# Layer 3 of the first batch: experts by scattered blocks instead of all experts for all tokens

## The reference

```python
qkv = xn @ w_qkv.T; q, k, v = split(qkv, 3)             # 64 wide, causal
s = softmax(mask(q @ k.T / 8)) @ v @ w_out.T + b_out
logits = xn @ router_w.T
topk_scores, topk_idx = top_k(logits + router_bias, 2)   # 2 of 16 experts
topk_scores = softmax(topk_scores)
hidden = silu(gate_all) * up_all                         # 16 experts, 64 hidden each
out = sum over the two experts of topk_scores * (hidden @ down)
out = out + (silu(xn @ sh_gate.T) * (xn @ sh_up.T)) @ sh_down.T
x = x + s * silu(out)
```

## Time and profile before

| what | us |
|---|---|
| median of three runs | 745.58 |
| span of the profiled execution | 753.9 |
| layer 3 of batch 0 | about 437.9 to 536.3 |
| layer 2 of batch 1 | about 536.3 to 659 |
| layer 3 of batch 1 | about 659 to the end |
| TensorE busy | 668.3 (89%) |
| VectorE busy | 433.6 (58%) |
| ScalarE busy | 365.3 (48%) |
| GpSimd busy | 196.9 (26%) |

### The profile page before, as it was taken

The page is one execution under the profiler, slowest core; times in us unless marked ns, Lnnn a source line. Parts: engine busy times, 40 slices in busy tenths (PEclk is TensorE's granted clock), DMA queues, the critical chain, the costliest instruction groups (busy, mean ns, idle before and its releaser), DMA issues. The chain is left out here.

```text
span 753.9 us, 12248 instructions
## 1 busy us (share of the span) xinstructions
PE 668.3 (89%) x4114; PEld 424.1 (56%) x4114; DVE 433.6 (58%) x940; ACT 365.3 (48%) x845; POOL 196.9 (26%) x194
## 2 busy tenths in 40 slices
PE   6899899994996899898998899899797998799896
PEld 2785434793783766665665654345365665645353
DVE  1826654561341753673575758765685486566654
ACT  4311683531661644356648643345348568453331
POOL 2000074036046100474555700000036334500000
PEclk9956997996998799996999999999999999999999
DMA  8800031252442431010000000000000000000000
GB/s 316 313 1 0 0 98 56 71 173 88 143 138 69 127 95 57 27 28 0 2 22 9 2 0 1 14 1 1 15 1 1 2 1 1 2 1 0 15 1 14
DMA packets 24044, 35.95 MB, mean 48 GB/s; under 512 B 2792, under 2 KB 14800, under 8 KB 23472
## 3 DMA queue, kind: packets, MB, share of 16 engines
q1 hardware_dynamic: 21008, 27.95, 11.2%
q0 software_dynamic: 2976, 7.21, 3.4%
HBM read 25.98 MB, written 9.18 MB: 47 GB/s over the span
## 5 line engine op out<-in xcount | busy, mean ns | idle before, releaser
L1157 ACT ACTIVATE arena<-bank 128x512 f32<-128x512 f32 (+8 forms) x224 | 125.7, 565 | 145.7 <-PE bank L544 63.8
L544 PE MATMUL bank<-arena,w 128*64 128x128 f32 (+2 forms) x528 | 150.1, 431 | 12.5 <-ACT arena L1157 6.6
L1157 ACT ACTIVATE arena<-bank,arena 128x128 f32<-128x128 f32 (+1 forms) x244 | 87.6, 386 | 108.5 <-PE bank L544 56.8
L544 PE MATMUL bank<-arena 64*128 64x256 f32 (+8 forms) x832 | 119.2, 346 | 2.4 <-ACT arena L1157 2.3
L544 PE MATMUL bank<-arena,work 128*128 128x128 f32 x624 | 88.2, 289 | 13.6 <-ACT arena L1157 4.7
L544 PEld LDWEIGHTS bank<-arena 64*128 64x128 f32 (+4 forms) x832 | 79.8, 181 | 31.8 <-issue 14.5
L544 PE MATMUL bank<-xn_b,w 128*128 128x512 f32 (+1 forms) x192 | 93.0, 608 | 4.8 <-DVE arena L2358 3.5
L544 PEld LDWEIGHTS bank<-arena,work 128*128 128x128 f32 x624 | 80.1, 200 | 27.5 <-issue 22.5
L544 PEld LDWEIGHTS bank<-arena,w 128*128 128x128 f32 (+1 forms) x528 | 62.4, 165 | 50.7 <-issue 34.8
L2448 POOL DMA_INDIRECT slots_in<-arena x32 | 33.8, 1055 | 99.1 <-ACT arena L1157 89.6
L544 PEld LDWEIGHTS bank<-xn_b,w 128*128 128x128 f32 (+1 forms) x192 | 35.0, 192 | 42.9 <-issue 29.5
(11 more groups left out here) (223 smaller groups left out, 912.8 us busy)
## 6 DMA issues: line engine op xcount, KB each, us to landing
work<-in_ew SPq DMA_DIRECT2D x46, 256.0 KB
slots_in<-work SPq DMA_DIRECT2D x2, 1472.0 KB, 17.4
arena<-slots_in SPq DMA_DIRECT2D x10, 256.0 KB, 4.1
slots_out<-arena POOLq DMA_DIRECT2D x10, 256.0 KB, 2.8
w_ew<-in_ew SPq DMA_DIRECT2D x1, 2048.0 KB, 11.7
w<-in_p SPq DMA_DIRECT2D x1, 1840.5 KB, 9.8
w<-in_p SPq DMA_DIRECT2D x1, 1297.0 KB, 10.5
w<-in_p SPq DMA_DIRECT2D x1, 1092.0 KB
```

The costliest lines, as they stand in the source:

```text
L544: return nc.tensor.matmul(o, lhsT, rhs, start=start, stop=stop, skip_group_check=True)
L1157: return nc.scalar.activation(o, i, f, bias=bias, scale=scale, **kw)
```

## The change

Layer 3 of batch 1 stays as it was. Layer 3 of batch 0 becomes `layer3_first`, and its experts leave it:

- `layer3_first` has 13 slots (`SLOTS3`). They hold the eight attention tiles, the shared expert of both groups, routing of both groups, `T1` and `N1` (table `SIDE3`), the transposes of the normalised tokens into rows (`rows_of`), a counting of tokens by expert (`counted`, nine matmuls) and, on VectorE, `dispatch3`: the place of each token's two rows in 31 blocks of 128, and a table of each block's expert (`table3`). The 16 routed experts are not computed there.
- GpSimd scatters 16 times 128 rows into `slots3_in` (DRAM) ahead of its layer-2 work of batch 1. SyncE blanks `slots3_in` at the start of the kernel.
- The 31 blocks are computed in eight groups of up to four (`experts3`, stream `X0`), ten advances, from within `layer2_att` of batch 1: after steps m = 2, 3, 4, 5, 6, 8 of g = 0 and m = 2, 4, 6, 8 of g = 1 (`X_AT`).
- Weights of each block come from DRAM, with register values read from `table3`.
- GpSimd gathers the results by token after its layer-2 work of batch 1, and a last stream `Y0` (`tail3`) forms batch 0's output inside `layer3(1)` of batch 1.

```diff
+X_AT = ((2, 3, 4, 5, 6, 8), (2, 4, 6, 8))
+Y_AT = (1, 2, 3, 4, 5)
...
+                def load_weights3(q):
...
+                    if q >= 2:
+                        sp.wait_ge(*at_of(0, "eo3", q - 2))
+                    for k in blocks3(q):
+                        e = nc.values_load(table3[0:1, 0, k:k + 1], engines=[mybir.EngineType.SP], min_val=0,
+                                           max_val=(E3 - 1) * H3)
+                        if q % 2:
+                            for a in range(2):
+                                sp.dma_start(ring3[1][:, k % SB3, (1 - a) * H3:(2 - a) * H3],
+                                             gate_up[:, a, bass.ds(e, H3)]).then_inc(ring3_in[1], 16)
+                        else:
+                            sp.dma_start(ring3[0][:, k % SB3].rearrange("p (a c) -> p a c", a=2),
+                                         gate_up[:, :, bass.ds(e, H3)]).then_inc(ring3_in[0], 16)
+                        half = nc.values_load(table3[0:1, 1, k:k + 1], engines=[mybir.EngineType.SP], min_val=0, max_val=1)
+                        pair = nc.values_load(table3[0:1, 2, k:k + 1], engines=[mybir.EngineType.SP], min_val=0,
+                                              max_val=(EP3 - 1) * D)
+                        sp.dma_start(dring3[sides3(q)[1], k % SB3],
+                                     downs[bass.ds(half, 1), :, bass.ds(pair, D)].rearrange("a h c -> (a h) c")).then_inc(
+                                         ring3_in[q % 2], 16)
...
+                for q in range(2):
+                    load_weights3(q)
+                sp.wait_ge(scattered3, 16 * 4 * C)
+                for q in range(2):
+                    load_slots3(q)
+                for q in range(NSB3 + 1):
+                    if q + 2 < NSB3:
+                        load_slots3(q + 2)
+                    if 1 <= q and q + 1 < NSB3:
+                        load_weights3(q + 1)
+                    if q:
+                        store_rows3(q - 1)
...
+                    def inward(q):
+                        o = fresh("quick", "gu3", q)
+                        pe.wait_ge(*at("cols3", q))
+                        pe.wait_ge(ring3_in[q % 2], (48 if q % 2 else 32) * sum(len(blocks3(j)) for j in range(q % 2, q + 1, 2)))
+                        for j, k in enumerate(blocks3(q)):
+                            i = mm(o[:, cs(j)], ring3[q % 2][:, k % SB3], cols3[:, q % 2, cs(j)])
+                        i.then_inc(*step("gu3", q))
+
+                    def outward(q):
+                        o = fresh("quick", "eo3", q)
+                        pe.wait_ge(*at("hx3", q))
+                        for j, k in enumerate(blocks3(q)):
+                            i = mm(o[:, cs(j)], hx3[sides3(q)[1], cs(j)], dring3[sides3(q)[1], k % SB3])
+                        i.then_inc(*step("eo3", q))
+                    for s in range(NSB3 + 2):
+                        if s < NSB3:
+                            turned(s)
+                        if 1 <= s <= NSB3:
+                            inward(s - 1)
+                        if s >= 2:
+                            outward(s - 2)
+                        yield
...
@@ layer2_att @@
+                        if now[1] and m in X_AT[g]:
+                            advance("X0")
```

More of the change, by code:

```diff
@@ L993, in entry3, with score3 @@
                     i.then_inc(*step("v3", g))
+                sums_at = {}
+                def score3(n):
+                    g = n // C
+                    halves = (n + 4) // 4
+                    pe.wait_ge(*at("k3", g))
+                    for k in range(halves):
+                        keys = min(GT, (n + 1) * CT - k * GT)
+                        o = fresh("quick", "s3", n, k)
+                        last = k == halves - 1
+                        half = slice(k * DK, (k + 1) * DK)
+                        i = mm(o[:, 0:keys], q3[half, n * CT:(n + 1) * CT], k3[half, k * GT:k * GT + keys],
+                               stop=not last)
+                        if last:
+                            i = mm(o[:, keys - CT:keys], identb[:], above[:], start=False)
+                        i.then_inc(*step("s3", n, k))
@@ new lines, in values3 @@
+                def values3(n):
+                    g, c = n // C, n % C
+                    if c == 0 and now[1] == 0:
+                        sums_at[g] = fresh("slow", "o3", g)
+                    for k in range((n + 4) // 4):
+                        pe.wait_ge(*at("pt3_s", n, k))
+                        for j in range(min(4, n + 1 - 4 * k)):
+                            i = mm(sums_at[g][:, c * DK:(c + 1) * DK], pt3[:, k, j], v3[:, 4 * k + j],
+                                   start=k == 0 and j == 0, stop=4 * k + j == n)
+                        i.then_inc(*step("pv3", n, k))
+                    if c == C - 1:
+                        reached[("o3", g)] = reached[("pv3", n, k)]
+                        growing.discard((now[1], "o3", g))
@@ new lines, in probs3 @@
+                def probs3(n):
+                    halves = (n + 4) // 4
+                    needs = [("mx3", n)]
+                    if n >= 2:
+                        needs.append(("pt3", n - 2, (n + 2) // 4 - 1))
+                    after(*needs)
+                    for k in range(halves):
+                        keys = min(GT, (n + 1) * CT - k * GT)
+                        fn(p3b[:, n % 2, k * GT:k * GT + keys], psum("s3", n, k)[:, 0:keys], ACT.Exp,
+                           bias=sm3[:, n, 0:1], accum_out=sm3[:, n, 1 + k:2 + k]).then_inc(
+                            *step("e3", n, k))
+                        reached[("s3", n, k, "read")] = reached[("e3", n, k)]
@@ new lines, in turned3 @@
+                def turned3(n):
+                    halves = (n + 4) // 4
+                    for k in range(halves):
+                        kc = min(4, n + 1 - 4 * k)
+                        after(("pt3", n, k), *([("pv3", n - 1, (n + 3) // 4 - 1)] if n else []))
+                        fn(pt3[:, k, 0:kc], psum("pt3", n, k)[:, 0:kc * CT].rearrange(
+                            "p (a b) -> p a b", b=CT), ACT.Copy).then_inc(*step("pt3_s", n, k))
+                        reached[("pt3", n, k, "read")] = reached[("pt3_s", n, k)]
@@ L2083, in entry2, with experts3, inner, evicted @@
                         pass
[L2085 removed]
+                def experts3():
+                    def inner(q):
+                        n = len(blocks3(q)) * P
+                        low, high = sides3(q)
+                        dve.wait_ge(*at("tg3x", q))
+                        if q == 0:
+                            dve.wait_ge(*at_of(1, "x", 2, 1))
+                        v.scalar_tensor_tensor(t3x[high, 0:n], tg3x[low, 0:n], 1.0, psum("gu3", q)[low, 0:n], ALU.add,
+                                               ALU.mult).then_inc(*step("t3x", q))
+                        after(*([("eo3", q - 2)] if q >= 2 else []))
+                        v.scalar_tensor_tensor(hx3[high, 0:n], t3x[high, 0:n], 0.5, psum("gu3", q)[high, 0:n], ALU.mult,
+                                               ALU.mult).then_inc(*step("hx3", q))
+                        reached[("gu3", q, "read")] = reached[("hx3", q)]
+                    def evicted(q):
+                        n = len(blocks3(q))
+                        dve.wait_ge(*at("eo3", q))
+                        if q >= 2:
+                            dve.wait_ge(rows3_out_sem[q % 2], 16 * (q // 2))
+                        v.tensor_copy(rows3_out[:, q % 2, 0:n], psum("eo3", q)[:, 0:n * P].rearrange(
+                            "p (b d) -> p b d", d=P)).then_inc(*step("rows3_out", q))
+                        reached[("eo3", q, "read")] = reached[("rows3_out", q)]
+                    for s in range(NSB3 + 2):
+                        if 1 <= s <= NSB3:
+                            inner(s - 1)
+                        if s >= 2:
+                            evicted(s - 2)
+                        yield
@@ L2087, in expert_blocks @@
+                advance = streams(dict(F=front, S=shared, C=nothing, M=mamba, T=tail, N=entry2, G=nothing, X=experts3,
+                                       Y=tail3), now)
                 def expert_blocks():
```

609 lines of the change are left out of this document (470 added, 139 removed).

## The result

The changed kernel takes 814.7 us (median of four runs, 808.8 to 823.1) against 745.3 for the kernel before: a ratio of 1.095 (95% interval 1.085 to 1.106). The direction of the forecast was right; its 765 us was 50 short and the range ended at 790. Some executions of most kernels are slower by some per cent at a lower granted clock (one each of e12 and e16 took over 1000 us), so medians here are of all executions and ratios with their intervals of the faster ones alone; for e3, e14 and e18, with two of those each, there is none.

What follows compares the result with a forecast made beforehand. TensorE was taken to bound layer 3 of batch 0, SyncE's weight loads to decide. 753.9 - 44 + 18 - 2 + 39.9 + 5 + 3 = 773.8 us of span, by 0.989: 765 us, range 730 to 790.

Steps and rivals of the forecast that it cites:

- What bounds it, and where the change is decided: TensorE bounds layer 3 of batch 0; SyncE's new weight loads in batch 1's attention decide the change.
- 1, dense experts removed: Layer 3 of batch 0: removing the experts saves 49.3 us of TensorE and 33 us of VectorE work.
- 2, what is left in layer 3 of batch 0: The stage falls from 98.4 to 54 us, -44 (-50 to -36); staying over 70 would show the prediction wrong.
- 3, the blocks: Batch 1's attention: 31 blocks add 18.0 us of TensorE work, of which 2 fall into existing waits.
- 4, the stalls: Batch 1's attention: five waits for SyncE's weight loads cost 39.9 us (30.4 with low prices, 56.8 with high).
- 5, the clock: Batch 1's attention: after stalls TensorE runs at a slower granted clock, costing 0 to 12 us, taken +5.
- Rival (b): From the third advance on the clock may stay at 1.2 GHz: +20 us more, 785 us; chance 0.10.
- 6, batch 0's output: Batch 1's layer 3: transposes and VectorE work for batch 0's output cost +3 us (1 to 5).
- 7, scatter and gather at nothing: GpSimd's scatter fits barely before layer-2 work, uncovered at most 5 us; gather has time before its reader; taken at nothing.
- The scaling by 0.989: Whole kernel: median of runs over profiled span, 745.58 to 753.9, turned 773.8 us of span into 765.
- Rival (a): Weight loads are hidden if a block takes SyncE under 2.0 to 2.3 us: 718 us; chance 0.20 with partial forms.
- What a measurement can tell, 0.3%: Whole kernel: a measurement can tell about 0.3% from no change; a result within that had chance 0.04.

Runs made afterwards that it cites:

- e12: The kernel before, with 16 indirect DMAs of 128 rows on GpSimd back to back at each layer 3, for which nobody waits: 768.8 us, 1.042.
- e16: The kernel before, with the softmax of both batches' layer 3 taken without its maximum: 735.8 us, ratio 0.988.
- e3: The changed kernel with 23 dummy matmuls in layer 3 of batch 0, before scores, transposes and the last output: 815.8 us.
- e14: The kernel before, with 16 plain DMAs of 128 rows issued by GpSimd at the start of each layer 3: 749.2 us (before 745.1).
- e18: The kernel before, with indirect DMAs of 128 rows in pairs, each pair waiting for the next expert unit of layer 3: 746.3 us (before 740.2).
- e11: The changed kernel with the softmax in layer 3 of batch 0 taken without its maximum: 796.1 us, ratio 1.075.
- e5: The changed kernel without GpSimd's 16 scattering and 16 gathering indirect DMAs: 799.6 us, ratio 1.080.
- e9: The changed kernel with 8 dummy matmuls in layer 3 of batch 0, one ahead of each tile's transposes: 820.9 us, ratio 1.103.
- the spread version: The changed kernel with early unchecked group reads, no maximum in either layer 3, and the ten advances spread five and five: 754.5 us, 1.014.
- e2: The changed kernel with dummy matmuls on TensorE before the gate-up matmuls of groups with stalls: 801.9 us, ratio 1.077.
- e1: The changed kernel with block weights read from fixed places, so SyncE reads no values: 774.4 us, ratio 1.042.
- e8: The changed kernel with a group's values in three reads of four ahead of the wait, without range checks: 781.7 us, ratio 1.050.
- e17: The kernel before, with 32 indirect DMAs of 16 rows on GpSimd, 16 back to back at each layer 3: 775.7 us, ratio 1.047.
- e13: The kernel before, with 16 plain DMAs of 128 rows on SyncE's queue at the start of each layer 3: 742.1 us, ratio 0.996.

## Why the prediction was wrong

- **What bounds it, and where the change is decided:** right. The load of weights stalls TensorE at the five places named, and it is the largest loss.
- **1, dense experts removed:** not the failing step; what was behind them is.
- **2, what is left in layer 3 of batch 0, 54 us (48 to 62):** the first step that failed, and one of its own signs of being wrong (over 70 us) came true: 81.2 us. I summed each slot as the larger of two engines' work and took the chain of a tile (3 us) as covered by the next slots' work. The slots 0 to 8 took 54 us for my 40, the last four 27 for 14. Leaving out the maximum takes 15 us off (e11), the scatter costs 3 to 4 (e5), the clock some 1 (e9); some 7 us more were not taken apart.
- **3, the blocks, +18 and -2:** in the spread version a full group's pieces at full clock are 0.60, 1.16 and 1.16 us, starting 0.51 and 1.09 apart, some 2.7 us where I had 2.32: 21 us for 31 blocks. No run shows the -2.
- **4, the stalls, +39.9 (30.4 to 56.8):** right; 32.9. The prices of a block were a little low (3.1 and 3.5 us for 2.92 and 3.30), the landing a little high (the last loads of the first two groups land 2.1 and 2.2 us after their issue, for my 2.4), and the intervals longer than I had them; the half clock and the blocks' own chain would lengthen them, which is argued and not shown. My 0.66 us for a value runs from the read's start to its DMA; the read's own row has 0.27.
- **5, the clock, +5:** its place was right, and no run contradicts its size; the clock fell in many more stretches (layer 3 at 0.70) where it cost little. Rival (b), a clock that costs 20 us more, isn't what made up the rest: lifting it to 0.85 took 3.4 us off the stage (e2).
- **Layer 2's remainder, not in the sum:** even with 6.9 us of waits (e1) the stage takes 160.0 us, of which 122.4 are the old work and 21 the blocks. About 10 us are left over, perhaps steps lengthened by the blocks between them; spreading did not take them away, and their cause is open.
- **6, batch 0's output, +3:** right, 3.4 (e5).
- **7, scatter and gather at nothing:** the second step that failed. I asked whether GpSimd had time for them, and it had. But they hold up the other engines: 3.2 and 13.5 us in the profiled executions (8 for the gather against the median of nine), 1.4% of the whole by the ratios, against the "at most 5" that I allowed the scatter. That they stood so close together was on view in the kernel before.
- **The scaling by 0.989:** it took the profiled execution of before as long in proportion. It was longer in its first 420 us only, so the factor took 9 us off that the change did not give back.
- **Rival (a), loads hidden, 718 us:** e8 brings a block to 1.3 and 1.9 us, below my break-even of 2.0 to 2.3, and is at 781.7; even no blocks at all is at 736.7. The break-even rested on steps 2 and 7, which failed.
- **What a measurement can tell, 0.3%:** too fine. The executions of a kernel differ by more, and the intervals here are 0.5% to 1.5% to either side.

The stages are 27, 14 and 14 us over the forecast's (layer 3 of batch 0, layer 2, layer 3 of batch 1), 54 in all. (With the median of the nine executions the last of them would be 8.) The slow start of before's profiled execution takes 18 off, the factor adds 9, what lies around the span 2, and the median over the profiled execution 3: the 50 us.

## What to carry to other kernels

When dense work is taken away, sum the stage again as a chain for each tile, not as the larger of the engines' work: what the dense work covered becomes the stage. For register-driven loads read the values of a whole group at once and ahead of the wait; and price an indirect DMA by what a burst does to the other engines, keeping it in small, spaced groups. Look for such bursts, and for engines that stand still behind them, in the kernel that you start from.

## What the hardware showed beyond the forecast

- 16 indirect DMAs back to back on GpSimd lengthened a stage with nothing that depends on them by 11.5 and 11.7 us (e12); with 16 rows instead of 128 by 16.1 and 11.1 (e17); in spaced pairs by 0.0 (e18); as plain DMAs on GpSimd by 0.0 and 1.6 (e14), on SyncE by 0.0 (e13).
- Three reads of four values ahead of the loads, in place of three reads for each block among them, brought SyncE from 3.1 to 1.3 us an even block (e8); the range checks made no difference (782.1 and 781.7 us).
- Dummy matmuls lifted the granted clock from 0.63 to 0.85 and from 0.70 to 0.85 or 0.88, and bought 3.4 us of a stage of 197 (1.6% of the whole by the medians, intervals overlapping) and nothing that shows: in these stages a chain through other engines or SyncE set the pace.
